# Routing weights broadcast through memory, and the next image's row turns moved in beside the last expert chunks

## The chip, the cores and the metric

The kernel runs on one core of one Trainium2 chip. The metric is the time of one execution in device microseconds (us), as the median of several runs. The profile is of one further execution of the same program and gives its span, from the first instruction to the last. TensorE's granted clock is shown beside it, 1.00 being 2.4 GHz and 0.50 being 1.2 GHz.

## What is computed

Eight images of 56 x 56 tokens with 64 channels pass through two layers. Cut to what matters here:

```python
# layer 0, mixing: y[i] = sum_j relu(xn[i] . xn[j])^2 * t[j], per image
sim = jnp.power(jax.nn.relu(jnp.einsum('bic,bjc->bij', xn, xn)), 2.0)
y = jnp.einsum('bij,bjc->bic', sim, t)
# layer 0, experts: 16 experts of 128, two chosen per token, computed for all tokens
dispatch = jnp.sum(jax.nn.one_hot(top_idx, n_experts) * top_probs[..., None], axis=-2)
hidden = jax.nn.silu(h1) * h2                       # h1, h2: 64 -> 128 for each expert
expert_out = jnp.einsum('bseh,eho->bseo', hidden, w3)
out = jnp.einsum('bseo,bse->bso', expert_out, dispatch)
# layer 1: a deformable 3x3 convolution (nine gathered taps a token, four corners each),
# then a feed-forward layer on the half of the tokens that a router picks, with gelu
```

Each sublayer has a layer norm before it and a skip around it. The routing weights are `dispatch`, one number per token and expert.

## The kernel before, in words

Every engine has an instruction list of its own, written out by hand and run in order. Semaphores tie the lists together (`pe.wait_ge(s["hid_done"], n)` holds the PE list until DVE has made n hidden tiles). The work is in three stages per image `k`:

- **Mixer** (`mixer`, two halves): `sims` makes similarities on PE, `relu_step` on ACT, squares on ACT and DVE, `mix` sums them on PE. It reads the normed rows of image `k` in three channel-major stacks, `xn_hl`, `xn_hh` and `xn_ll` (float16, high and low parts). The geometry of image k-1's convolution (`geo_prepare`), the feed-forward preparation of image k-2 (`ffn_prepare`) and convolution samples are threaded between its steps.
- **Gate**: logits, softmax and the two largest on DVE (`gate`, 26 small steps with drains between), then the feed-forward of image k-2. At its end DVE splits `disp` into a high and a low float16 half (`dsplit`, L891 to L893), PE turns them to channel-major rows (25 transposes in 7 groups) and ACT copies these into `dT` (L1482).
- **Experts** (`experts_chunk`): the 3136 tokens go in 7 chunks `c` (512, 384, 512, 384, 512, 384, 448 tokens), 16 experts `e` in each. Step `e` of the PE list waits for `hid_done` of expert `e`, issues `up(e + 2)` (four matmuls into banks S), a convolution sample's piece of image k-1 at even steps, and at odd steps the down matmuls of an expert pair (L1543 `PS<-work,w3s`), then `spread(p + 1)` (one matmul with `pick` that repeats two experts' routing weights over 64 rows each, into bank Y1) and `collect(p - 1)` (L1747, transposes that accumulate the weighted output into D1). Step `e` of the ACT list does `silu(e)` (L1435), a sample's copy, and at odd steps copies Y1 to `share` (L1441). Step `e` of the DVE list makes `hid(e)` (L908), at odd steps multiplies the pair's output by `share` (`scale_pair`, L904), and weighs gathered corners (`weigh`, L490 to L498). Pieces of the next image's norm (`norm_piece`) fill both lists.

`up(e + 2)` writes the banks that `hid(e)` has read, so PE runs up to two experts ahead of DVE:

```python
for e in range(E):
    pe.wait_ge(s["hid_done"], n0 + e + 1)
    if e + 2 < E:
        up(e + 2, c)
```

After the last chunk, `stacks` turns image k+1's normed rows: 21 groups of 3 or 4 transposes on PE (75 in all) through four banks, and 21 copies on ACT (`evac_tr`, L1281). Beside it DVE runs `geo_start(k)`: row sum, mean, centring, square and row sum over all 25 tiles (L458, L510, L645, L647, L458). The next `mixer` follows. Gathers for the convolution are issued by POOL (L452, nine a tile, two tile buffers `G`). SP issues the other DMAs: the corner table of image k-1, the stored skip of image k-2, the load of image k+1 and the store of `yw`, each behind its own semaphore.

## Time and profile before

| | |
|---|---|
| median of 3 runs | 4166.61 us (4163.04 to 4169.43) |
| profiled execution, span of the core | 4159.1 us |
| profiled execution, time outside the span | not recorded; the median run is 7.5 us above the span |
| mean granted TensorE clock | 0.900 |
| PE, DVE, ACT, POOL busy | 85%, 74%, 58%, 47% of the span |
| experts of image 1 | 663.7 to 880.4 us |
| turning of image 2's rows | 880.4 to 890.1 us |

The middle images repeat with a period of about 461.5 us: the experts of image 1 start at 663.7 and its last collect ends near 880.4, and the same places of image 2 lie near 1125 and 1342. A row's first number is the start, its second the duration; "[0.89 <-DVE work L908]" says that the engine was idle 0.89 us before and that DVE's L908 ended it. A busy PE is a PE with matmuls in flight, and matmuls overlap, so a matmul's slot is the distance to the next start.

### The profile page before, as it was taken

How to read it: one execution, taken by the hardware profiler on the slowest of the kernel's cores; microseconds unless marked ns; L12 is line 12 of the kernel's file. 1: busy time of each engine (PE TensorE's matmuls, PEld its weight loads, DVE VectorE, ACT ScalarE, POOL GpSimd, SP SyncE). 2: the span in 40 equal slices, each digit the busy share in tenths (PEclk: the TensorE clock that was granted, in tenths of full speed). 3: DMA queues.
4: the chain of work that ended last, by engine and by line, in shares of the span. 5: the costliest groups of instructions: out<-in, count | busy, mean ns of one | idle time of the engine just before them, and what ended most of it. 6: DMA issues, size and time to landing. Idle time of an engine off the chain costs nothing.

```text
span 4159.1 us, 58338 instructions
## 1 busy us (share of the span) xinstructions
PE 3515.1 (85%) x21688; PEld 1896.4 (46%) x21688; DVE 3096.5 (74%) x4894; ACT 2399.5 (58%) x4152; POOL 1974.2 (47%) x1805
## 2 busy tenths in 40 slices
PE   5979997999899999999889999999899999946431
PEld 2434444454544445444544455444544455525321
DVE  6466477887788687877788678877688678865775
ACT  5755774577655775577556775577556775522210
POOL 0000074554456364555455463545455464657670
PEclk8989998999899999999899989999899989965555
DMA  4000122232222332231222332232222332234355
GB/s 112 1 8 1 40 82 67 74 99 56 71 83 80 78 89 64 75 98 58 79 77 74 79 96 56 77 92 64 74 79 70 81 86 65 83 103 117 101 123 113
DMA packets 374811, 314.92 MB, mean 76 GB/s; under 512 B 312672, under 2 KB 317024, under 8 KB 374528
## 3 DMA queue, kind: packets, MB, share of 16 engines
q0 software_dynamic: 85248, 231.33, 19.0%
q1 hardware_dynamic: 289280, 79.88, 8.9%
q8 instruction: 171, 2.80, 0.3%
q14 instruction: 112, 0.92, 0.1%
HBM read 279.30 MB, written 57.69 MB: 81 GB/s over the span
## 4 chain that ended last, share of the span: by engine, by line
PE 63%; DVE 16%; ACT 9%; DVEq 5%; issue 3%; DMA 2%; SPq 1%; POOL 1%; ACTq 0%
PE PS L1543 57%; DVE work L908 3%; PE PS L1747 3%; DVEq L492 3%; DVE G L496 2%; PE PS L1579 2%; DVE G L490 2%; DVE small L904 1%; ACT work L1363 1%; ACT work L1435 1%; ACT small L1408 1%; PE PS L1583 1%; ACT xn_hl L1281 1%; POOL G L452 1%; DMA out<-x 1%
## 5 line engine op out<-in xcount | busy, mean ns | idle before, releaser
L452 POOL DMA_INDIRECT G<-corner_table,index x1800 | 1973.6, 1096 | 2049.0 <-DVE values L498 737.5
L1435 ACT ACTIVATE work<-PS,descale 128x512 f32<-128x512 f32 (+2 forms) x896 | 566.7, 633 | 514.9 <-PE PS L1543 503.5
L1363 ACT ACTIVATE work<-PS 128x768 f32<-128x768 f32 (+2 forms) x800 | 651.1, 823 | 273.4 <-PE PS L1543 222.6
L908 DVE SCALAR_TENSOR_TENSOR work<-PS,descale,work 128x512 f32<-128x512 f32 (+2 forms) x896 | 605.7, 680 | 152.3 <-ACT work L1435 138.3
L818 DVE TENSOR_TENSOR work<-work 128x768 f32<-128x768 f32 (+2 forms) x496 | 480.1, 972 | 294.9 <-PE PS L1543 252.4
L1543 PE MATMUL PS<-work,xm 128*64 128x400 f32 (+3 forms) x3200 | 622.3, 502 | 0.0
L490 DVE TENSOR_TENSOR G<-G,corner_w 128x768 f32<-128x768 f32 x600 | 561.4, 951 | 43.5 <-DMA G<-corner_table,index 42.1
L1543 PE MATMUL PS<-xn_hl,xn_hh 128*128 128x384 f16 (+2 forms) x1600 | 539.2, 337 | 51.0 <-ACT work L1363 42.3
L1543 PE MATMUL PS<-xn_hl,xn_ll 128*128 128x384 f16 (+2 forms) x1600 | 534.0, 334 | 0.0
L1543 PE MATMUL PS<-work,w3s 128*64 128x384 f32 (+2 forms) x1792 | 439.8, 569 | 64.5 <-DVE small L904 64.5
L1543 PE MATMUL PS<-xn_hl,w1h 128*128 128x512 f16 (+2 forms) x896 | 319.5, 357 | 64.2 <-DVE work L908 55.6
L1441 ACT ACTIVATE small<-PS 128x512 f32<-128x512 f32 (+2 forms) x448 | 242.9, 542 | 214.4 <-PE PS L1543 211.5
L1543 PEld LDWEIGHTS PS<-xn_hl,xn_hh 128*128 128x128 f16 (+1 forms) x1600 | 158.3, 99 | 379.1 <-ACT work L1363 187.8
L1543 PEld LDWEIGHTS PS<-work,xm 128*64 128x64 f32 (+1 forms) x3200 | 232.1, 136 | 192.8 <-issue 159.0
L1543 PE MATMUL PS<-xn_hl,w2h 128*128 128x512 f16 (+2 forms) x896 | 318.1, 355 | 0.0
L1543 PE MATMUL PS<-xn_hl,w1l 128*128 128x512 f16 (+2 forms) x896 | 318.1, 355 | 0.0
L1543 PE MATMUL PS<-xn_hl,w2l 128*128 128x512 f16 (+2 forms) x896 | 317.8, 355 | 0.0
L904 DVE TENSOR_TENSOR small<-PS,small 128x512 f32<-128x512 f32 (+2 forms) x448 | 275.5, 615 | 31.0 <-PE PS L1543 31.0
L496 DVE TENSOR_TENSOR G<-G 128x1152 f32<-128x1152 f32 x200 | 272.6, 1363 | 18.2 <-issue 0.4
L1287 ACT ACTIVATE val_cm<-PS 128x512 f32<-128x512 f32 x200 | 118.1, 591 | 283.8 <-PE PS L1579 283.8
L1392 ACT ACTIVATE work<-work 128x768 f32<-128x768 f32 (+3 forms) x304 | 259.7, 854 | 2.6 <-PE PS L1543 2.2
L1579 PE MATMUL PS<-ident,values 128*128 128x128 f32 x800 | 139.0, 303 | 142.1 <-DVE xB L503 112.5
(262 smaller groups left out, 4961.2 us busy)
## 6 DMA issues: line engine op xcount, KB each, us to landing
G<-corner_table,index POOLq DMA_INDIRECT x1800
corner_table<-rows_scratch SPq DMA_DIRECT2D x32, 784.0 KB
corner_table<-G SPq DMA_DIRECT2D x8, 841.0 KB, 8.5
xin<-x SPq DMA_DIRECT2D x8, 768.0 KB, 5.7
rows_scratch<-xln SPq DMA_DIRECT2D x8, 768.0 KB
x_scratch<-xB SPq DMA_DIRECT2D x8, 768.0 KB
yw_scratch<-yw SPq DMA_DIRECT2D x7, 784.0 KB, 6.4
x<-x_scratch SPq DMA_DIRECT2D x4, 784.0 KB, 6.0
```

What stands on the lines that cost most here:

```text
L452: GP.indirect_dma_start(G[0:rows, n % 2, tap * 4 * C:(tap + 1) * 4 * C], None, tables[b % 2], bass.IndirectOffsetOnAxis(ap=index[0:rows, c ...
L490: V.tensor_tensor(g, g, bc(w, 2, C), ALU.mult)
L496: V.tensor_tensor(g[:, :, 0:2, :], g[:, :, 0:2, :], g[:, :, 2:4, :], ALU.add)
L818: V.tensor_tensor(sq[0:rows, u % 4, :, 0:n], relu[0:rows, u % 2, :, 0:n], relu[0:rows, u % 2, :, 0:n], ALU.mult).then_inc(s["sq_dve"], 1)
L904: V.tensor_tensor(scaled_y[:, p % 2, 0:w], Y0[:, 0:w], share[:, p % 2, 0:w], ALU.mult).then_inc(s["scaled_done"], 1)
L908: V.scalar_tensor_tensor(hid[:, e % 4, 0:w], S[2 + e % 2][:, 0:w], descale[:, MOE2:MOE2 + 1], silu[:, e % 2, 0:w], ALU.mult, ALU.mult).the ...
L1363: A.activation(relu[0:rows, u % 2, :, 0:n], PS[u % 2][0:rows, :, 0:n], ACT.Relu).then_inc(s["relu_done"], 1)
L1392: A.activation(sq[0:rows, u % 4, :, 0:n], relu[0:rows, u % 2, :, 0:n], ACT.Square).then_inc(s["sq_act"], 1)
L1435: A.activation(silu[:, e % 2, 0:w], S[e % 2][:, 0:w], ACT.Silu, scale=descale[:, MOE1:MOE1 + 1]).then_inc(s["silu_done"], 1)
L1441: A.activation(share[:, e // 2 % 2, 0:w], Y1[:, 0:w], ACT.Copy, scale=1.0 / XS).then_inc(s["share_ready"], 1)
L1543: return P.matmul(o, a, b, start=start, stop=stop, skip_group_check=True)
L1579: ins = P.transpose(D0[:, i * TP:(i + 1) * TP], value[:, i * 128:(i + 1) * 128], ident[0:TP, 0:TP])
```

## The change

Two things are changed.

**Routing weights.** `spread`, `pick`, `dsplit` and the ACT copies of Y1 are gone. PE turns `disp` itself, in float32 (25 `P.transpose`), ACT copies it to `share_cm` (16 rows), SP stores that to DRAM in two pieces (`share_out`) and, for each of the 56 expert pairs of an image, loads two rows back, each broadcast over 64 partitions (`share_back`, two DMAs of up to 128 KB), into four buffers in turn; a buffer is loaded again when `scale_pair` four pairs earlier is done. DVE's `scale_pair` waits for these DMAs. The scale of the up product moves into the routing weight, so `hid` is a two-operand multiply.

**Row turns.** The 21 groups of the next image are no longer behind the last chunk. Group `i` stands at one step (chunk, expert) of `STACK_STEPS`: two in chunk 4, twelve in chunk 5, seven in chunk 6. PE issues it after `up(e + 2)` and the sample's piece, into bank Y1, and ACT copies it at the end of its own step `e`. The token rows have two buffers (`token_cm`), by the image's parity. The first two `sims` of the next image come before the last `collect`. `geo_start` is split: three of four quarters of sum, centring and squares lie in chunks 5 and 6 (the squares on ACT), the last quarter after the last chunk.

```diff
+STACK_STEPS = ((4, 13), (4, 15), *((5, e) for e in (1, 2, 3, 5, 6, 7, 9, 10, 11, 13, 14, 15)), *((6, e) for e in (1, 2, 3, 5, 6, 7, 9)))
@@ SP
+            def share_back(k, p):
+                c, e, n = p // (E // 2), 2 * (p % (E // 2)), k * (NCH * E // 2) + p
...
+                if n >= 4:
+                    sp.wait_ge(s["scaled_done"], n - 3)
+                for b in range(2):
+                    sp.dma_start(share[n % 4][b * C:(b + 1) * C, 0:width(c)],
+                                 share_dram[e + b:e + b + 1, span(c)].to_broadcast([C, width(c)])).then_inc(share_in[n % 4], 16)
@@ SP, image(k)
+                share_out(k)
+                for p in range(NCH * E // 2):
+                    share_back(k, p)
+                    if k >= 2 and p == E // 2 - 1:
+                        store_yw(k - 2)
@@ DVE
+                    if (c, e) == ((5, 2), (5, 6), (5, 8))[q]:
+                        geo_sum(i, quarter(q))
+                    if (c, e) == ((5, 10), (5, 14), (6, 0))[q]:
+                        geo_center(i, q)
+                    if (c, e) == ((6, 6), (6, 8), (6, 10))[q]:
+                        ln_square_sum("g", i, tmp, 0, q)
...
             def geo_start(i):
...
+                geo_sum(i, quarter(3))
+                geo_center(i, 3)
...
-                tt(disp[:, :, :], o1, o2, ALU.add)
-                V.tensor_copy(dsplit[:, :, 0:E], disp[:, :, :])
-                dve.drain()
-                V.tensor_tensor(dsplit[:, :, E:2 * E], disp[:, :, :], dsplit[:, :, 0:E], ALU.subtract).then_inc(s["disp_split"], 1)
+                V.tensor_tensor(disp[:, :, :], o1, o2, ALU.add).then_inc(s["disp_done"], 1)
...
-                    V.scalar_tensor_tensor(hid[:, e % 4, 0:w], S[2 + e % 2][:, 0:w], descale[:, MOE2:MOE2 + 1], silu[:, e % 2, 0:w],
-                                           ALU.mult, ALU.mult).then_inc(s["hid_done"], 1)
+                    V.tensor_tensor(hid[:, e % 4, 0:w], S[2 + e % 2][:, 0:w], silu[:, e % 2, 0:w], ALU.mult).then_inc(s["hid_done"], 1)
@@ ACT, experts_chunk: behind silu(e) and a sample's copy
-                    if e % 2:
-                        act.wait_ge(s["share_done"], p0 + e // 2 + 1)
-                        A.activation(share[:, e // 2 % 2, 0:w], Y1[:, 0:w], ACT.Copy, scale=1.0 / XS).then_inc(s["share_ready"], 1)
...
+                    if k + 1 < B and (c, e) in STACK_STEPS:
+                        i = STACK_STEPS.index((c, e))
...
+                        evac_stack(k + 1, i, Y1)
@@ ACT, image(k), behind the experts
-                if k + 1 < B:
-                    stacks(k + 1, 0, 3 * NCH)
-                ln_std("g", k, 0)
+                square("g", k, tmp, xln, 3)
@@ PE, experts_chunk
+                    if k + 1 < B and (c, e) in STACK_STEPS:
+                        next_stack(k + 1, STACK_STEPS.index((c, e)))
...
-                        pe.wait_ge(s["share_ready"], p0 + p + 1)
-                        if p + 1 < E // 2:
-                            spread(p + 1, c)
...
-                    spread(0, c + 1)
-                    up(0, c + 1)
+                    up(k, 0, c + 1)
+                elif k + 1 < B:
+
+                    pe.wait_ge(s["n_cm"], (k + 2) * 3 * NCH)
+                    sims(k + 1, 0, 0, 0)
+                    sims(k + 1, 0, 0, 1)
@@ PE, gate
-                        ins = mm(S[c % 4][0:2 * E, i * TP:i * TP + rows], dsplit[0:rows, t, :], ident16[0:rows, 0:rows])
+                        ins = P.transpose(S[c % 4][0:E, i * TP:i * TP + rows], disp[0:rows, t, :], ident[0:rows, 0:rows])
```

The PE list of image 1, chunk 5, steps 6 and 7, before (`xn_hl,w1h` begins an up, `work,w3s` is the down, `ident,small` the collect; lines and queues have other numbers in the changed file):

```order
L1543 MATMUL PS0<-xn_hl,w1h 128x384 [waits hid_done]
L1543 MATMUL PS0<-xn_hl,w1l 128x384
L1543 MATMUL PS1<-xn_hl,w2h 128x384
L1543 MATMUL PS1<-xn_hl,w2l 128x384
L1543 MATMUL PS2<-work,w3s 64x384 [waits scaled_done]
L1543 MATMUL PS2<-work,w3s 64x384
L1543 MATMUL PS2<-xn_hh,pick 128x384 [waits share_ready]
L1747 MATMUL PS3<-ident,small 128x128 x3
```

and with the change, both steps (`ident16,split` is a group of row turns):

```order
L1604 MATMUL PS0<-token_cm1,w1h 128x384 [waits hid_done]
L1604 MATMUL PS0<-token_cm1,w1l 128x384
L1604 MATMUL PS1<-token_cm1,w2h 128x384
L1604 MATMUL PS1<-token_cm1,w2l 128x384
L1604 MATMUL PS2<-ident16,split 128x128 [waits n_cm,n_split]
L1604 MATMUL PS2<-ident16,split 128x128 x3
L1604 MATMUL PS0<-token_cm1,w1h 128x384 [waits hid_done]
L1604 MATMUL PS0<-token_cm1,w1l 128x384
L1604 MATMUL PS1<-token_cm1,w2h 128x384
L1604 MATMUL PS1<-token_cm1,w2l 128x384
L1604 MATMUL PS2<-ident16,split 128x128 [waits n_cm,n_split]
L1604 MATMUL PS2<-ident16,split 128x128 x3
```

A group of turns now stands between a step's up and the next step's wait for `hid_done`, and the spread is gone. (The first fence is step 7 alone; step 6 was its first four rows.)

The ACT list at the same place (silus are `work<-PS0,descale`), from the group of step 6 to the silu of step 10, with the change:

```order
L1332 ACTIVATE token_cm0<-PS2 128x512 [waits n_tr]
L1493 ACTIVATE work<-PS0,descale 128x384 [waits up_done]
L1332 ACTIVATE xn_stacks<-PS2 128x512 [waits n_tr]
L1493 ACTIVATE work<-PS0,descale 128x384 [waits up_done] x2
L1332 ACTIVATE xn_stacks<-PS2 128x512 [waits n_tr]
L1493 ACTIVATE work<-PS0,descale 128x384 [waits up_done]
```

Each copy of a group lies between the silu of its own step and the silu of the next.

The PE list at the end of image 1's last chunk, with the change (`zero16` opens the mixer):

```order
L1604 MATMUL PS0<-token_cm0,xn_stacks 128x384 [waits n_cm]
L1604 MATMUL PS0<-token_cm0,xn_stacks 128x384 x3
L1604 MATMUL PS1<-token_cm0,xn_stacks 128x384 x4
L1811 MATMUL PS3<-ident,small 128x128 [waits scaled_done]
L1811 MATMUL PS3<-ident,small 128x128 x2
L1811 MATMUL PS3<-ident,small 64x128
L1604 MATMUL PS2<-zero16 128x384 x2
```

Before, the last collect came first, then the 75 turns, then these similarities.

## Rows read from the trace of the kernel before

**Rows 1.** The page, section 1: busy time, share of the span, instructions.

```profile
PE 3515.1 (85%) x21688; PEld 1896.4 (46%) x21688; DVE 3096.5 (74%) x4894; ACT 2399.5 (58%) x4152; POOL 1974.2 (47%) x1805
```

**Rows 2.** Image 1's experts: busy PE, PEld, DVE, ACT, POOL, PEclk, DMA; waits.

```profile
663.00:880.00 217.00, 201.46 (x1135) 103.61 (x1136) 188.41 (x295) 119.93 (x212) 121.78 (x118) 0.98 0.24 72
...
PE PS L1543 <- DVE small L904: 8.7, 7, 2.6
PE PS L1543 <- DVE work L908: 5.9, 10, 0.9
```

**Rows 3.** Instruction groups, PE: spread, gate's turns (busy us, mean ns, idle before).

```profile
L1543 PE MATMUL PS<-xn_hh,pick 128*128 128x512 f16 (+2 forms) x448 | 163.5, 365 | 0.0
...
L1543 PE MATMUL PS<-ident,dsplit 128*32 128x128 f16 (+1 forms) x200 | 19.9, 261 | 31.9 <-DVE dsplit L893 30.9
```

**Rows 4.** Timeline, PE, image 1, chunk 5, steps 6 to 8.

```profile
835.39 0.33 PE L1543 MATMUL PS<-xn_hl,w1h 128*128 128x384 f16 x1
...
836.04 0.33 PE L1543 MATMUL PS<-xn_hl,w1h 128*128 128x384 f16 x1
...
837.58 0.34 PE L1543 MATMUL PS<-xn_hh,pick 128*128 128x384 f16 x1
837.76 0.49 PE L1747 MATMUL PS<-ident,small 128*128 128x128 f32 x3
838.09 0.33 PE L1543 MATMUL PS<-xn_hl,w1h 128*128 128x384 f16 x1
```

**Rows 5.** Timeline, same chunk, ACT and DVE: a silu, its hid, a scale_pair.

```profile
841.17 0.55 DVE L904 TENSOR_TENSOR small<-PS,small 128x384 f32<-128x384 f32 x1
...
842.06 0.58 ACT L1435 ACTIVATE work<-PS,descale 128x384 f32<-128x384 f32 x1 [0.49 <-PE PS L1543]
...
842.68 0.62 DVE L908 SCALAR_TENSOR_TENSOR work<-PS,descale,work 128x384 f32<-128x384 f32 x1
```

**Rows 6.** Timelines of PE, ACT and DVE, from image 1's experts to image 2's mixer.

```profile
880.39 8.58 PE L1543 MATMUL PS<-ident,split 128*128 128x128 f16 x75
890.14 0.34 PE L1543 MATMUL PS<-xn_hl,xn_hh 128*128 128x384 f16 x1 [1.17 <-ACT xn_ll L1281]
...
880.81 0.60 ACT L1281 ACTIVATE xn_hl<-PS 128x512 f16<-128x512 f32 x1 [1.58 <-PE PS L1543]
881.31 0.59 ACT L1281 ACTIVATE xn_hh<-PS 128x512 f16<-128x512 f32 x1
...
882.26 0.51 ACT L1281 ACTIVATE xn_hl<-PS 128x384 f16<-128x384 f32 x1
882.63 0.53 ACT L1281 ACTIVATE xn_hh<-PS 128x384 f16<-128x384 f32 x1
...
891.00 1.51 ACT L1363 ACTIVATE work<-PS 128x768 f32<-128x768 f32 x2 [0.81 <-PE PS L1543]
...
881.60 1.82 DVE L458 TENSOR_REDUCE st<-xB 128x25 f32<-128x1600 f32 x1
```

**Rows 7.** Timelines at image 1's gate: PE, DVE.

```profile
659.95 2.90 PE L1543 MATMUL PS<-ident,dsplit 128*32 128x128 f16 x25 [15.44 <-DVE dsplit L893]
663.74 0.61 PE L1543 MATMUL PS<-xn_hl,w1h 128*128 128x512 f16 x1 [0.89 <-ACT xn_hh L1482]
...
658.68 0.57 DVE L891 CAST dsplit<-small 128x400 f16<-128x400 f32 x1
```

**Rows 8.** Busy by stretch around a lull of PE inside image 1's mixer.

```profile
499.90:503.30 3.40, 1.12 (x8) 0.31 (x4) 0.50 (x2) 3.33 (x13) 0.00 (x0) 1.00 0.00 0
503.30:506.70 3.40, 3.32 (x22) 1.18 (x22) 2.09 (x5) 2.38 (x4) 0.00 (x0) 0.50 0.00 0
```

**Rows 9.** A 128 KB load; POOL's waits in 663 to 880; DVE in the tail.

```profile
work<-pick_in SPq DMA_DIRECT2D x1, 128.0 KB, 2.4
...
POOL G L452 <- DVE values L498: 72.5, 14, 27.1
...
3684.97 2.70 DVE L490 TENSOR_TENSOR G<-G,corner_w 128x768 f32<-128x768 f32 x3 [9.18 <-DMA G<-corner_table,index]
```

More of the change, by code:

```diff
@@ L636, in nothing, with geo_sum, geo_center, geo_early @@
             def nothing(): pass
-            def geo_start(i):
-                x2 = xB[i % 2]
-                dve.drain()
-                ln_sum(x2[:, :, :], 0)
-                ln_mean(0)
-                if i > 0:
-                    dve.wait_ge(s["rows_written"], i * 32)
-                V.tensor_tensor(xln[:, :, :], x2[:, :, :], bc(st[:, 0, 1, :], 2, C), ALU.subtract)
-                dve.drain()
-                V.tensor_tensor(tmp[:, :, :], xln[:, :, :], xln[:, :, :], ALU.mult)
-                dve.drain()
-                red(st[:, 0, 2, :], tmp[:, :, :])
-                ln_var("g", 0, LNC_EPS)
+            def geo_sum(i, r):
+                dve.drain()
+                red(st[:, 0, 0, r], xB[i % 2][:, r, :])
+            def geo_center(i, q):
+                r = quarter(q)
+                if q in (0, 3):
+                    all_in = slice(0, quarter(2).stop) if q == 0 else r
+                    dve.drain()
+                    V.tensor_scalar(st[:, 0, 1, all_in], st[:, 0, 0, all_in], 1.0 / C, None, ALU.mult)
+                    dve.drain()
+                if q == 0 and i > 0:
+                    dve.wait_ge(s["rows_written"], i * 32)
+                ln_center("g", xln, xB[i % 2], 0, q)
+            def geo_early(i, c, e):
+                for q in range(3):
+                    if (c, e) == ((5, 2), (5, 6), (5, 8))[q]:
[4 more added lines that the diff above has]
+                        ln_square_sum("g", i, tmp, 0, q)
+            def geo_start(i):
+                geo_sum(i, quarter(3))
+                geo_center(i, 3)
             def ffn_sum(f):
@@ L1329, in offsets_tm, with geo_early @@
                 taken(slice(18, 27), ACT.Sigmoid).then_inc(s["om_taken"], 1)
+            def geo_early(i, c, e):
+                for q in range(3):
+                    if (c, e) == ((5, 15), (6, 1), (6, 3))[q]:
+                        square("g", i, tmp, xln, q)
             def geo_prepare(i, j, u):
+                if (j, u) == (0, 0):
+                    ln_std("g", i, 0)
                 for q in range(4):
-                    if (j, u) == ((0, 1), (0, 2), (0, 4), (0, 7))[q]:
+                    if (j, u) == ((0, 2), (0, 4), (0, 5), (0, 7))[q]:
                         cast_h("g", i, 0, q)
@@ L1450, in gelu_chunk, with evac_stack @@
                                  bias=fb1c[:, m:m + 1], scale=descale[:, FFN1:FFN1 + 1]).then_inc(s["gelu_done"], 1)
-            def stacks(k, i0, i1):
-                for i in range(i0, i1):
-                    c = i // 3
-                    evac_tr("n", k * 3 * NCH, i, (xn_hl, xn_hh, xn_ll)[i % 3][:, span(c)], S[i % 4][:, 0:width(c)])
+            def evac_stack(k, i, bank):
+                c = i // 3
+                evac_tr("n", k * 3 * NCH, i, (normed(k), xn_hh, xn_ll)[i % 3][:, span(c)], bank[:, 0:width(c)])
             def image(k):
@@ L1481, in image @@
                     act.wait_ge(s["disp_tr"], k * NCH + c + 1)
-                    A.activation(dT[0:2 * E, span(c)], S[c % 4][0:2 * E, 0:width(c)], ACT.Copy).then_inc(s["disp_cm"], 1)
+                    A.activation(share_cm[:, span(c)], S[c % 4][0:E, 0:width(c)], ACT.Copy).then_inc(s["disp_cm"], 1)
                 for c in range(NCH):
@@ L1556, in transpose_map, with first_stacks, next_stack @@
                 ins.then_inc(s["g_tr"], 1)
-            def stacks(k, i0, i1):
-                if i0 == 0:
-                    pe.wait_ge(s["n_split"], 4 * k + 4)
-                for i in range(i0, i1):
+            def first_stacks():
+                pe.wait_ge(s["n_split"], 4)
+                for i in range(3 * NCH):
                     if i >= 4:
-                        pe.wait_ge(s["n_cm"], k * 3 * NCH + i - 3)
+                        pe.wait_ge(s["n_cm"], i - 3)
                     transpose_chunk("n", S[i % 4], i // 3, (C, 0, 2 * C)[i % 3])
-                if i1 == 3 * NCH:
-                    pe.wait_ge(s["n_cm"], (k + 1) * 3 * NCH)
+                pe.wait_ge(s["n_cm"], 3 * NCH)
+            def next_stack(k, i):
+                if i == 0 and k >= 3:
+                    pe.wait_ge(s["fout_read"], k - 2)
+                pe.wait_ge(s["n_split"], 4 * k + quarters_of(i // 3))
+                if i:
+                    pe.wait_ge(s["n_cm"], k * 3 * NCH + i)
+                transpose_chunk("n", Y1, i // 3, (C, 0, 2 * C)[i % 3])
             def sample(b, t, stage):
@@ L1653, in ffn_prepare, with sims @@
                         ffn_transpose(f, c)
-            def sims(half, j, u):
+            def sims(k, half, j, u):
                 rows, n = tile_rows(j), IWS[half]
```

121 lines of the change are left out of this document (67 added, 54 removed).

## The prediction, made before the change was run

> **What bounds the kernel now.** I read the page first [rows 1]: PE is busy 85% of the span, DVE 74%, ACT 58%, POOL 47%. PE leads, but a share over the whole span does not say what an edit of one stage is worth, so I went to the stage that is changed. In the experts of image 1 [rows 2] PE is busy 201 of 217 us at a clock of 0.98, DVE 188, ACT 120. PE's waits there are 8.7 + 5.9 us, so the stage lasts as long as PE's instruction slots. DVE is close behind. The timeline of two steps shows the same [rows 4]: step 6 takes 836.04 - 835.39 = 0.65 us, which is its four up matmuls back to back; step 7 takes 838.09 - 836.04 = 2.05 us and holds up, down, spread and collect without a pause that another engine ends. PE can run so because the ups are two experts ahead: silu and hid of the next expert are made while PE does this one. Between the experts and the next mixer, PE, ACT and DVE all change work [rows 6]: the turns start at 880.39, the first similarities at 890.14, the first relu at 891.00.
>
> **The change, part by part.** An execution of 4159.1 us is the base; the median of the runs shown is 7.5 us above it.
>
> *Spread.* 448 matmuls go [rows 3]. One slot at 384 columns is 837.76 - 837.58 = 0.18 us [rows 4], by columns 0.22 at 512, on average 0.20. Fourteen of an image's 56 lie in steps that also get a group of turns and are priced there; the 42 others give 8.2 us in each of images 0 to 6 and the last image gives 10.9: 68 us. PE is the bound but DVE's 188 of 217 us is near [rows 2], so I count 85% of it, **-58 us**. The ACT copies of Y1 lie beside PE work, and go at no gain. Hid loses an operand and goes from 0.62 to about the 0.55 of a two-operand multiply of that size [rows 5]; DVE is not the bound, so that is worth nothing where PE leads.
>
> *Turns inside the steps.* Here I expect the loss. The group of step e is issued after up(e + 2). ACT copies it at the end of its own step e, so ahead of silu(e + 1); hid(e + 1) waits for silu(e + 1); and PE's step e + 1 begins with a wait for hid(e + 1). The two-expert lead is gone in such a step, and the engines take turns. The length of one such round, for 384 tokens: up 0.65 [rows 4]; from the group's first transpose to the start of its copy 880.81 - 880.39 = 0.42 [rows 6]; from that copy to the next ACT instruction 0.50 at 512 columns and 0.37 at 384 [rows 6]; silu 0.58, then 842.68 - 842.64 = 0.04 to hid, hid 0.55, and 0.04 again to PE [rows 5]. That is 2.78 us, or 2.60 with a group of three tiles (0.37 + 0.37 in place of 0.42 + 0.50), half of each in chunk 5: 2.69. It is 2.04 more than an even step and 0.64 more than an odd one, spread included. Chunk 5 has groups at even steps 2, 6, 10, 14 and odd steps 1, 3, 5, 7, 9, 11, 13 that pay (15 hides in the wait at the chunk's end): 8.2 + 4.5 = 12.7 us. Chunk 6 has two even and five odd: 4.1 + 3.2 = 7.3. In chunk 4 only step 13 pays, about 0.4. That is 20.3 us an image and, for the seven images that have a next one, **+142 us**. Sample pieces lengthen a step on both sides alike. The step after such a row (4, 8, 12) has lost its lead as well: DVE must weigh (0.90 each, 2.70 for three [rows 9]) and make hid, some 1.5 us, where PE needs 0.8; about 1.5 us an image, **+9 us**.
>
> *Boundary.* The 9.75 us between 880.39 and 890.14 go. What is late next is the geometry's last quarter: after the last collect DVE adds the output twice (it takes until 881.60, when the row sum starts [rows 6]), then a quarter of sum and centring, about 0.6 each by a quarter of 1.82 plus the start, and a small step; ACT squares, 0.6, and only then takes the first relu. So relu starts near 883.7. The eight similarities now ahead of the last collect push it by 0.9. The relu comes 891.0 - 884.6 = 6.4 us earlier, seven times, **-45 us**. But PE then has nothing for some 3 us. In the mixer of image 1 a stretch of 3.4 us with 1.1 us of PE work was followed by 3.4 us at clock 0.50 [rows 8], and 3.4 us at half clock is at most 1.7 us of lost work: **+12 us** for seven. After image 7 the shorter geo_start (it now makes a quarter of it in place of all: four passes of 1.82 [rows 6], 7.3 us, become about 2.5) lies on the path to the tail: **-5 us**.
>
> *Gate.* In float32 a turn has a slot of (838.09 - 837.76) / 3 = 0.11 us at full clock [rows 4], twice that at half: 2.75 or 5.5 us for 25, against 2.90 before [rows 7] and some 3.1 for ACT's copies beside them. The two DVE steps for dsplit (658.68 to 659.95, 1.27 us) go, but PE waited for them 30.9 us in all [rows 3], 15.4 of it in image 1, so in images 0 and 1 alone. I take +0.9 for each of these two and +0.3 for the six others: **+4 us**.
>
> *Broadcasts.* 56 pairs an image, two loads of up to 128 KB each. One load of 128 KB took 2.4 us [rows 9]. A pair is wanted every 2.7 to 3.9 us and four buffers lie ahead, so a pair has over 10 us: nothing on the path. SP has little else to issue meanwhile. The bounds are from nothing to 2.4 us more on each of 56 pairs, far off. What could be hit is the gathers: POOL waited 72.5 us of 217 for DVE [rows 9], so that much slack covers them; I take 0. The Trainium skill ("DMA: Bandwidth & Descriptors", section "Issuing engines are not separate DMA queues") says that DMAs of all issuers share the same 16 engines and interleave. By that rule the broadcasts slow the gathers; the trace agrees in the tail, where the table's write held DVE for 9.18 us on a gather [rows 9]. It is a rival below.
>
> *Clock in the rounds.* PE is at work in about half of a round, less in even steps. If the clock stays at 1.00 this costs nothing; if it is at 0.50 all through, each of 21 rounds has up and turns twice as long, +0.85 us, 125 us for seven images. The stretch in [rows 8] was emptier (a third) than a round, so I stay near the lower end: **+12 us**.
>
> Sum: -58 + 142 + 9 - 45 + 12 - 5 + 4 + 12 = **+71 us**, 4230 for the profiled execution's span and 4238 against the median.
>
> **The rivals.**
> 1. *The rounds don't form* (faster). PE would need a copy that finds ACT idle and a silu that does not wait, so that a group costs only its own slots, at most 0.42 us by 21 groups, under 9 us an image. Then: spread -87 (all of it), turns at most +55, boundary and clock -33, tail and gate -1: 66 less, 4100. For it speaks that ACT is busy only 120 of 217 us; against it the two lists, in which the copy stands ahead of silu(e + 1). It decides when a round costs less than half of my 0.97 us mean excess: 147 rounds by 0.48 are 71 us. That half-way case is no change.
> 2. *Gathers are late.* The experts move 72 GB/s at a DMA share of 0.24 [rows 2]; the broadcasts add some 12.8 MB in 217 us, 59 GB/s. In the tail at a high share a gather came 9 us late [rows 9]. If one of two tiles an image-chunk comes 2 us late beyond POOL's slack, 14 tiles an image by 2 us by 3 to 7 images: 60 to 100 more, about 4320.
> 3. *Half clock in the rounds*, as worked out: 4238 + 113 = about 4350.
> 4. *The first pair of an image is late*, by at most two DMAs of 2.4 us each way: under 5 us by 8. It only widens the range.
>
> **How the numbers follow.** My forecast has 0.68, rival 1 0.13 (with 0.06 more for the half-way case), rival 2 0.06, rival 3 0.07. What a measurement here can tell from no change is 0.2%, 8 us. Slower: 0.68 + 0.06 + 0.07 = 0.81; same 0.05; faster 0.14, part of the half-way case being on either side. The forecast's own range is 4205 to 4280 (85 to 100% of the spread, rounds between 2.5 and 2.9 us, clock between 0 and 40 us). To hold 8 in 10 the range goes down to 4160, the half-way case, and up to 4305; it leaves out rival 1 and the upper part of 2 and 3.
>
> **What would show it.** In the changed profile: PE steps of chunk 5 that carry a group near 2.7 us, with PE idle before each up and DVE's hid named as what ended it, and chunk 5 some 13 us longer than before; chunks 0 to 3 shorter by 1 to 1.7 us each; first relu about 4 us behind the last collect, PEclk at 0.50 just after; no DVE wait for share DMAs. I am wrong if chunk 5 keeps its length (rival 1), if weigh waits for gathers in the experts (rival 2), or if PEclk in chunks 5 and 6 is far below 1 (rival 3).

## The result, and the profile after

The changed kernel takes 4253.3 us (median of 4 runs, 4248.7 to 4261.5) against 4168.0 us (4 runs, 4163.0 to 4170.9): ratio 1.0205, 95% interval 1.019 to 1.0221, so 79 to 92 us slower. Forecast were 4238 us and 71 us slower, in a range of 4160 to 4305.

Section 1 of the changed kernel's page answers to [rows 1]; under it the rows on clock and DMA (tenths, 40 slices) and on the hardware queue's share:

```profile
PE 3497.6 (82%) x21240; PEld 1876.7 (44%) x21240; DVE 3021.2 (71%) x4948; ACT 2174.2 (51%) x3736; POOL 1971.7 (46%) x1805
...
PEclk8989998999899999999899998999899999965555
DMA  4021124432353333432353333432353333443445
...
q1 hardware_dynamic: 361424, 184.17, 17.3%
```

Every engine has less to do than before, PE too, and the span is 90.7 us longer (4249.9 against 4159.1). So the loss is waiting, not work. The waits of the whole run name it, of PE before:

```profile
PE PS L1543 <- DVE small L904: 64.5, 56, 3.0
PE PS L1543 <- DVE work L908: 55.6, 89, 1.2
```

and after (L961 is the line that makes `hid`, L908 before):

```profile
PE PS L1604 <- DVE work L961: 177.2, 203, 2.0
...
PE PS L1604 <- ACT work L1422: 62.9, 59, 3.7
PE PS L1604 <- DVE small L957: 58.5, 55, 2.6
```

(A row of waits gives the total in us, the number of waits and the longest.) PE waits for `hid` 203 times in place of 89, and 177.2 us in place of 55.6. To see where, I cut both spans at the starts of PE's `w1h` matmuls, of which there is one for each image, chunk and expert. The forecast's terms are put beside the stages they belong to (the gate's term lies between the images); differences are of unrounded times:

| stage, us | before | after | difference | forecast |
|---|---|---|---|---|
| chunks 0 to 4, eight images | 1249.0 | 1206.4 | -42.6 | -49 |
| chunk 5, eight images | 213.6 | 323.1 | +109.4 | |
| chunk 6 to its last up, eight images | 197.4 | 269.3 | +71.9 | 5 and 6: +154 |
| from there to the next image's first up, seven | 1741.2 | 1697.0 | -44.2 | -29 |
| head and tail | 758.0 | 754.1 | -3.8 | -5 |

The round itself. Timelines of PE, ACT and DVE of the changed kernel, image 1, chunk 5, from up(8) to up(9), an even step with a group:

```profile
845.81 0.34 PE L1604 MATMUL PS<-token_cm,w1h 128*128 128x384 f16 x1 [0.37 <-DVE work L961]
...
846.47 0.39 PE L1604 MATMUL PS<-ident,split 128*128 128x128 f16 x4
848.61 0.34 PE L1604 MATMUL PS<-token_cm,w1h 128*128 128x384 f16 x1 [1.75 <-DVE work L961]
...
846.90 0.60 ACT L1332 ACTIVATE token_cm<-PS 128x512 f16<-128x512 f32 x1 [1.73 <-PE PS L1604]
847.39 0.57 ACT L1493 ACTIVATE work<-PS,descale 128x384 f32<-128x384 f32 x1
...
848.00 0.56 DVE L961 TENSOR_TENSOR work<-PS,work 128x384 f32<-128x384 f32 x1 [1.60 <-ACT work L1493]
```

Up from 845.81, turns from 846.47, copy at 846.90, silu at 847.39, hid at 848.00, PE again at 848.61: 2.80 us, where the same step took 0.65 before [rows 4]. PE waits for DVE, DVE for ACT and ACT for PE, so the five pieces of this chain follow one another and none lies beside another. The forecast had 2.78 for this round and 2.60 with three tiles; the latter measures 2.64 (median of images 1 to 6; 843.18 to 845.81 in this one).

The boundary, which answers to [rows 6]: PE, ACT and DVE after the last chunk of image 1.

```profile
911.33 0.60 PE L1811 MATMUL PS<-ident,small 128*128 128x128 f32 x4
911.77 0.49 PE L1604 MATMUL PS<-zero 128*128 128x384 f16 x2
915.91 1.36 PE L1604 MATMUL PS<-token_cm,xn_stacks 128*128 128x384 f16 x7 [3.65 <-ACT work L1422]
...
914.58 0.58 ACT L1323 ACTIVATE tmp<-xln 128x448 f32<-128x448 f32 x1 [6.09 <-DVE xln L550]
915.06 1.49 ACT L1422 ACTIVATE work<-PS 128x768 f32<-128x768 f32 x2
...
912.97 0.62 DVE L493 TENSOR_REDUCE st<-xB 128x7 f32<-128x448 f32 x1
913.67 0.17 DVE L684 TENSOR_SCALAR st<-st 128x7 f32<-128x7 f32 x1
913.92 0.63 DVE L550 TENSOR_TENSOR xln<-xB,st 128x448 f32<-128x448 f32 x1
```

The first relu (915.06) is 3.13 us behind the end of the last collect (911.33 + 0.60). Before, the last collect of image 1 was

```profile
879.89 0.66 PE L1747 MATMUL PS<-ident,small 128*128 128x128 f32 x4 [0.20 <-DVE small L904]
```

and the relu at 891.00 [rows 6] was 10.45 behind its end. The chain between is the one forecast: two additions, the quarter's sum, its mean, its centring, ACT's square, relu.

### The profile page after: what moved, and what is told of

The parts are those of the page before. It is cut to its first block, busy times and chain, and to the rows that moved or that the text cites. A ratio compares the mean times of both kernels' runs of the same rounds, so it can differ in the third digit from the quotient of the medians.

```text
span 4249.9 us, 58165 instructions
## 1 busy us (share of the span) xinstructions
PE 3497.6 (82%) x21240; PEld 1876.7 (44%) x21240; DVE 3021.2 (71%) x4948; ACT 2174.2 (51%) x3736; POOL 1971.7 (46%) x1805
## 4 chain that ended last, share of the span: by engine, by line
PE 58%; DVE 18%; ACT 10%; DVEq 5%; issue 4%; DMA 2%; POOL 1%; SPq 1%; ACTq 0%
PE PS L1604 52%; DVE work L961 5%; PE PS L1811 3%; DVEq L527 3%; ACT work L1493 2%; DVE G L525 2%; DVE G L531 2%; PE PS L1647 2%; DVE small L957 1%; POOL G L487 1%; ACT token_cm L1332 1%; ACT work L1422 1%; ACT xn_stacks L1332 1%; DVE st L493 1%; ACT small L1467 1%
## 5 line engine op out<-in xcount | busy, mean ns | idle before, releaser
L961 DVE TENSOR_TENSOR work<-PS,work 128x512 f32<-128x512 f32 (+2 forms) x896 | 551.7, 619 | 299.0 <-ACT work L1493 294.6
L1604 PE MATMUL PS<-token_cm,xn_stacks 128*128 128x400 f16 (+3 forms) x3200 | 628.6, 338 | 63.6 <-ACT work L1422 62.9
L1604 PEld LDWEIGHTS PS<-token_cm,xn_stacks 128*128 128x128 f16 (+1 forms) x3200 | 286.2, 100 | 478.4 <-ACT work L1422 208.1
L1604 PE MATMUL PS<-token_cm,w1h 128*128 128x512 f16 (+2 forms) x896 | 325.7, 363 | 155.4 <-DVE work L961 148.4
L1604 PE MATMUL PS<-token_cm,w1l 128*128 128x512 f16 (+2 forms) x896 | 323.0, 361 | 0.0
L1604 PE MATMUL PS<-token_cm,w2h 128*128 128x512 f16 (+2 forms) x896 | 321.9, 359 | 0.0
L1604 PE MATMUL PS<-token_cm,w2l 128*128 128x512 f16 (+2 forms) x896 | 320.8, 358 | 0.0
L1811 PEld LDWEIGHTS PS<-ident,small 128*128 128x128 f32 x1600 | 178.5, 145 | 304.7 <-issue 297.2
L1811 PE MATMUL PS<-ident,small 128*128 128x128 f32 x1600 | 282.8, 297 | 0.2 <-DVE small L957 0.2
L1604 PE MATMUL PS<-ident,split 128*128 128x128 f16 (+1 forms) x1224 | 143.0, 241 | 116.4 <-DVE split L1223 48.4
```

What stands on the lines that cost most here:

```text
L961: V.tensor_tensor(hid[:, e % 4, 0:w], S[2 + e % 2][:, 0:w], silu[:, e % 2, 0:w], ALU.mult).then_inc(s["hid_done"], 1)
L1604: return P.matmul(o, a, b, start=start, stop=stop, skip_group_check=True)
L1811: ins = P.matmul(D1[0:rows, n * 128:(n + 1) * 128], scaled_y[:, p % 2, n * TP:n * TP + rows], ident[:, :], start=p == 0 and n == 0, stop=p ...
```

## The experiments

Eleven kernels, each timed beside the kernel before on the same chip; the ratios are against that timing (medians of 4165.2 to 4170.5 us). The stages are those of the table above (head and tail, 750 to 761 us, left out). They are of the one profiled execution, which is not always the median one: with the copy one step later it took 4079.2 us, the shortest of four, with copy later and geometry at the end 4117.9, the longest.

| run | median, us | ratio to before | chunks 0 to 4 | chunk 5 | chunk 6 | between |
|---|---|---|---|---|---|---|
| before | 4168.0 | | 1249.0 | 213.6 | 197.4 | 1741.2 |
| changed kernel | 4253.3 | 1.019 to 1.0221 | 1206.4 | 323.1 | 269.3 | 1697.0 |
| copy one step later | 4088.9 | 0.9794 to 0.9827 | 1188.1 | 233.2 | 206.3 | 1700.1 |
| turns at the end | 4117.2 | 0.9857 to 0.989 | 1189.8 | 221.0 | 197.1 | 1754.5 |
| routing weights alone | 4098.9 | 0.9795 to 0.9853 | 1185.9 | 204.7 | 189.4 | 1758.2 |
| geometry at the end | 4274.6 | 1.0238 to 1.0272 | 1204.8 | 321.9 | 264.6 | 1727.4 |
| no broadcasts | 4262.8 | 1.0191 to 1.0242 | 1203.8 | 320.9 | 275.1 | 1710.3 |
| odd steps | 4218.3 | 1.0096 to 1.0138 | 1216.8 | 278.5 | 253.0 | 1713.4 |
| odd steps, copy later | 4087.4 | 0.9789 to 0.9824 | 1193.5 | 226.4 | 202.4 | 1705.4 |
| turns ahead of up | 4148.0 | 0.9944 to 0.9976 | 1194.8 | 260.2 | 224.8 | 1703.6 |
| copy later, geometry at the end | 4114.7 | 0.9858 to 0.9899 | 1188.3 | 230.8 | 202.4 | 1733.5 |
| geometry moved, first | 4096.9 | 0.9802 to 0.9841 | 1189.3 | 242.7 | 203.1 | 1708.4 |
| geometry moved, second | 4092.1 | 0.9806 to 0.9848 | 1187.9 | 232.3 | 205.7 | 1707.1 |

**The copy one step later.** ACT's copy of step e's group moves behind silu(e + 1); PE and DVE are as in the changed kernel.

```diff
-                    if k + 1 < B and (c, e) in STACK_STEPS:
-                        i = STACK_STEPS.index((c, e))
+                    if k + 1 < B and (c - (e == 0), (e - 1) % E) in STACK_STEPS:
+                        i = STACK_STEPS.index((c - (e == 0), (e - 1) % E))
```

> The changed kernel, but ACT copies the group of step e one step later, behind silu(e + 1) in place of ahead of it. Theory of the rounds (copy ahead of silu(e + 1) takes PE's lead away): chunks 5 and 6 of images 0 to 6, 181 us longer than before in the changed kernel, keep only the groups' own slots and the geometry's passes, some 40 to 60 us; steps with a group fall from 2.6 to 2.8 us to about 1.1 (even) and 2.3 (odd); in all 4253 - 130 = about 4125 us. Rival (a group costs its price wherever the copy stands: PE slots, a lower clock, DVE): within 30 us of 4253.

Measured 4088.9 us: 164 us less than the changed kernel and 79 us less than before. I had expected 128 less: chunks 5 and 6 keep 28.5 us over before, not 40 to 60, and chunks 0 to 4 give another 18 back, 16 of them in chunk 4. Of the 164 us an estimated 19 to 34 are the clock, which no longer falls in chunks 5 and 6 (worked out below). The same step in its trace, from up(8) to up(9), and a step on:

```profile
812.94 0.34 PE L1604 MATMUL PS<-token_cm,w1h 128*128 128x384 f16 x1
...
813.60 0.39 PE L1604 MATMUL PS<-ident,split 128*128 128x128 f16 x4
814.05 0.34 PE L1604 MATMUL PS<-token_cm,w1h 128*128 128x384 f16 x1
...
816.26 0.33 PE L1604 MATMUL PS<-token_cm,w1h 128*128 128x384 f16 x1
...
814.03 0.60 ACT L1332 ACTIVATE token_cm<-PS 128x512 f16<-128x512 f32 x1 [1.48 <-PE PS L1604]
...
813.45 0.55 DVE L961 TENSOR_TENSOR work<-PS,work 128x384 f32<-128x384 f32 x1
```

The hid that PE needs for its next step starts at 813.45, while PE is still in this one, and up(9) follows the turns with no wait: 1.11 us in place of 2.80. The odd step takes 2.21 (814.05 to 816.26), and 1.92 is an odd step's length with neither spread nor group (same chunk, routing weights alone). So a group costs 0.46 and 0.29 us here, about its slots, and no round forms. PE's waits for hid over the run fall back to what they were before:

```profile
PE PS L1604 <- DVE work L961: 57.5, 92, 1.2
```

One position in ACT's list is thus the whole loss, and more: the other parts of the change are a gain.

**Turns at the end; routing weights alone.** The first takes `next_stack` and `evac_stack` out of the steps and puts them behind the last chunk, through four banks (PE's part is shown; ACT's copies move likewise):

```diff
                 for c in range(NCH):
                     experts_chunk(k, c)
+                if k + 1 < B:
+                    pe.wait_ge(s["n_split"], 4 * k + 8)
+                    for i in range(3 * NCH):
+                        if i >= 4:
+                            pe.wait_ge(s["n_cm"], (k + 1) * 3 * NCH + i - 3)
+                        transpose_chunk("n", S[i % 4], i // 3, (C, 0, 2 * C)[i % 3])
+                    pe.wait_ge(s["n_cm"], (k + 2) * 3 * NCH)
+                    sims(k + 1, 0, 0, 0)
+                    sims(k + 1, 0, 0, 1)
```

> The changed kernel with all 21 groups of row turns back behind the last chunk, through four banks; the geometry's passes stay in the steps, the weights still go through memory. Rounds theory: chunks 5 and 6 lose their 181 us and gain the spread's slots (20 us) less the geometry's passes on DVE (about 16 us); the boundary takes back some 7 us seven times, 50 us: 4253 - 181 - 4 + 50 = about 4115 us. If the weights' way through memory cost something (gathers late, waits for the loads) this would stay above 4150.

The second does so as well and has the geometry at the end too:

```diff
             def geo_start(i):
-                geo_sum(i, quarter(3))
-                geo_center(i, 3)
+                for q in range(4):
+                    geo_sum(i, quarter(q))
+                for q in range(4):
+                    geo_center(i, q)
...
-                square("g", k, tmp, xln, 3)
+                for q in range(4):
+                    square("g", k, tmp, xln, q)
```

> As the run before, and the geometry's four sums, centrings and squares also back behind the last chunk: what is left of the change is the weights' way through memory. By my terms (spread -58, gate measured at -4) about 4168 - 62 = 4106 us, so a little below the run before (its geometry passes cost 2.3 us in chunk 5 of the last image, where there are no turns; times eight is 18, less 3 in the tail). If geometry passes are free in the steps, this run is no faster than the one before or slower.

Measured 4117.2 and 4098.9 us, expected 4115 and 4106. With the routing part alone, chunks 0 to 6 are 80.0 us shorter than before: 0.179 us for each of the 448 spreads, 90% of the slot of 0.20. What lies between the images is 17 us longer there, and why is not shown. Half of it stands in the gate, where in both kernels the clock is low for some 27 us an image; over all that lies between the images, the clock rows hold 290 us at half clock against 254 before, which may be a part of it. The two runs also bring out a cost that the forecast did not have: with the geometry's passes in the steps, chunks 5 and 6 are 24.0 us longer (221.0 + 197.1 against 204.7 + 189.4). In the first of the two, images 1 to 6 also have 3.4 us each at half clock in these chunks, the second has none, so some us of the 24 are the clock's.

From here the row turns' account can be made without the rest. Against the kernel with the turns at the end, the changed one has +191 us in the steps (+16.6, +102.1, +72.2) and -57.5 between the images: +133. With the later copy it is +20 in the steps and -54 between: -35 (-28 by the medians).

**Geometry at the end**, the turns left in the steps (the diff is the second one above, on the changed kernel):

> The changed kernel with the geometry's sums, centrings and squares all behind the last chunk; the turns stay in the steps. First relu later: three more quarters of sum and centring on DVE, 3.6 us, and ACT's squares, so the boundary is about 3.5 us longer, seven times, and the tail 5 us: +30. Against it, chunk 5 loses the passes: -16 if they are on the path beside the rounds, 0 if the rounds hide them. So 4267 (on the path) or 4283 us (hidden).

Measured 4274.6 us, 21 more, half-way between the two expected. The first relu is 3.7 us later, seven times, 26.2 us; chunks 5 and 6 together are 5.9 us shorter. So the rounds hide most of the passes, and these make up some 6 us of the loss at most.

**No broadcasts** from image 1 on:

```diff
-                    share_back(k, p)
+                    if k == 0:
+                        share_back(k, p)
...
-                    dve.wait_ge(share_in[n % 4], 32 * (n // 4 + 1))
+                    if k == 0:
+                        dve.wait_ge(share_in[n % 4], 32 * (n // 4 + 1))
```

> The changed kernel with the broadcasts and DVE's waits for them left out from image 1 on (the weights of images 1 to 7 are then stale values of the four buffers, so the routing weights are wrong in them). If the 12.8 MB an image hide beside the rest, as forecast: within 8 us of 4253. If they hold up the gathers (rival 2): faster by 20 us or more, and POOL's gathers and DVE's wait for them shorter.

Measured 4262.8 us (4250.7 to 4267.3): not faster, with 90 MB less to move. (The two intervals overlap; its profiled execution has 21 us more at half clock in chunks 5 and 6, and 31 more between the images.) Its page and a row of POOL's waits in the experts of image 1 (676 to 911), then the same wait of the changed kernel there:

```profile
q1 hardware_dynamic: 298704, 94.20, 10.0%
...
POOL G L488 <- DVE values L534: 85.6, 12, 26.6
```

```profile
POOL G L487 <- DVE values L533: 90.8, 13, 26.4
```

POOL waits for DVE about as long with the broadcasts as without, so it has slack in both. The gathers do land a little later: from the issue of a tile's last gather to the last landing the median of 200 tiles is 3.18 us in the changed kernel, 2.84 without broadcasts and 2.93 before. POOL's slack covers these 0.3 us. The offsets that steer the gathers are worked out from wrong values in this run, so its gathers may read other addresses; the kernel before, with the right ones, gives nearly the same figure. A broadcast of 128 KB took 3.2 us from issue to landing, the four buffers give it over 10, and DVE never waits for one in the changed kernel's trace.

**Odd steps.** The order on ACT is that of the changed kernel, but 19 of the 21 groups stand in odd steps in place of 15:

```diff
-STACK_STEPS = ((4, 13), (4, 15), *((5, e) for e in (1, 2, 3, 5, 6, 7, 9, 10, 11, 13, 14, 15)), *((6, e) for e in (1, 2, 3, 5, 6, 7, 9)))
+STACK_STEPS = (*((4, e) for e in (9, 11, 13, 15)), *((5, e) for e in (1, 3, 5, 7, 8, 9, 11, 13, 15)), *((6, e) for e in (1, 3, 5, 7, 8, 9, 11, 13)))
```

> The changed kernel, ACT's copy still ahead of the next silu, but 19 of the 21 groups at odd steps (from step 9 of chunk 4 on) in place of 15. Rounds theory: a round is 2.6 to 2.8 (3.05 in chunk 6) whatever the step, so four fewer even steps (0.65 to 2.8) and four more odd ones (2.05 to 2.8) are worth 4 x 1.4 x 7 = 39 us: about 4215 us. A fixed price of a group: no change, within 10 us of 4253.

Measured 4218.3 us, for 4215 by the theory of the rounds. The steps bear it out: in chunk 5 an odd step with a group now takes 2.63 to 2.80 us (medians of images 1 to 6) and the one even step (step 8) went from 1.10 to 3.24. A round is as long wherever it forms, and in an odd step more of it was there already. That the total fits so well is luck in part: the steps lost 50 us and the stretches between the images gained 16, and chunks 5 and 6 have 10 us at half clock in place of 86, which the theory had left out. A fixed price for a group, with the clock's gain added, would give nearly the same total; the lengths of the steps and the next run speak against it.

**Odd steps and the later copy** together:

> The odd steps of the run above and the later copy together. In the later-copy kernel an even step with a group is 0.46 us longer than one without, an odd one 0.3 to 0.46; so where a group stands should matter no more once no round forms: within 12 us of the later-copy kernel's 4089. Rival (even steps are dearer for another reason, such as DVE's work in them): 20 us or more below it.

Measured 4087.4 against 4088.9 us, no difference. Once no round forms, the place of a group does not matter.

**Turns ahead of up.** ACT as in the changed kernel; on PE the group goes ahead of the step's up:

```diff
                     pe.wait_ge(s["hid_done"], n0 + e + 1)
+                    if k + 1 < B and (c, e) in STACK_STEPS:
+                        next_stack(k + 1, STACK_STEPS.index((c, e)))
                     if e + 2 < E:
                         up(k, e + 2, c)
...
-                    if k + 1 < B and (c, e) in STACK_STEPS:
-                        next_stack(k + 1, STACK_STEPS.index((c, e)))
```

> The changed kernel, ACT's copy still ahead of silu(e + 1), but PE issues the group of a step ahead of up(e + 2) in place of behind it. Rounds theory: the up (0.65) then runs beside the copy, and the round from hid to hid is turns 0.42 + copy 0.50 + silu 0.58 + 0.04 + hid 0.55 + 0.04 = 2.13 us. An even step with a group goes from 2.8 to about 2.15, an odd one is again bound by PE's own slots, about 2.35: six even groups by 0.65 and fourteen odd ones by 0.35 are 8.8 us an image, 62 us: about 4190. If what holds the next step were not this chain but, say, the group's wait for its bank, the order of the two would not matter: within 10 us of 4253.

Measured 4148.0 us: 105 less than the changed kernel, where I expected 62. Timelines of PE, ACT and DVE of the same even step:

```profile
825.43 0.40 PE L1604 MATMUL PS<-ident,split 128*128 128x128 f16 x4
825.66 0.33 PE L1604 MATMUL PS<-token_cm,w1h 128*128 128x384 f16 x1
...
827.58 0.40 PE L1604 MATMUL PS<-ident,split 128*128 128x128 f16 x4 [1.10 <-DVE work L961]
827.81 0.33 PE L1604 MATMUL PS<-token_cm,w1h 128*128 128x384 f16 x1
...
829.74 0.33 PE L1604 MATMUL PS<-token_cm,w1h 128*128 128x384 f16 x1
...
825.86 0.60 ACT L1332 ACTIVATE token_cm<-PS 128x512 f16<-128x512 f32 x1 [1.48 <-PE PS L1604]
826.36 0.57 ACT L1493 ACTIVATE work<-PS,descale 128x384 f32<-128x384 f32 x1
...
826.96 0.56 DVE L961 TENSOR_TENSOR work<-PS,work 128x384 f32<-128x384 f32 x1 [0.95 <-ACT work L1493]
```

The round is turns, copy, silu, hid, 825.43 to 827.58: 2.15 us, forecast 2.13, with the up now beside the copy. The odd step behind it takes 2.16, from its own group at 827.58 to the next step's up at 829.74, where I had 2.35. Fourteen such steps by 0.19 are an estimated 19 us over seven images; that, and the clock (below, an estimated 15 to 30 us), is why it gained more.

**Geometry at the end with the later copy:**

> The later-copy kernel with the geometry's sums, centrings and squares all behind the last chunk. Its two prices are known from runs: in the steps they cost 24 us where no rounds hide them, behind the last chunk they hold the first relu up by 3.7 us seven times, 26 us. So no difference from the later-copy kernel, within 10 us of 4089; chunks 5 and 6 shorter by about 3 us an image, the relu later by 3.7.

Measured 4114.7 us, 26 more: a miss. The 24 us that the passes cost with the turns at the end are 6 here (chunk 5 2.4, chunk 6 3.9), and there is no half clock in these chunks in either run. Between the images 33 us come in the two profiled executions, 26 of them the later relu. A price found beside one neighbour did not hold beside another. Why is not shown; that PE's slots for the turns cover DVE's passes would fit.

**The geometry's passes moved** to where DVE was seen idle, on the later-copy kernel, twice. The first move (the second is ((5, 3), (5, 6), (5, 11)), ((6, 0), (6, 2), (6, 3)), and ((6, 1), (6, 4), (6, 5)) on ACT):

```diff
-                    if (c, e) == ((5, 2), (5, 6), (5, 8))[q]:
+                    if (c, e) == ((5, 3), (5, 4), (5, 11))[q]:
...
-                    if (c, e) == ((5, 10), (5, 14), (6, 0))[q]:
+                    if (c, e) == ((5, 12), (6, 2), (6, 3))[q]:
...
-                    if (c, e) == ((6, 6), (6, 8), (6, 10))[q]:
+                    if (c, e) == ((6, 10), (6, 11), (6, 12))[q]:
...
-                    if (c, e) == ((5, 15), (6, 1), (6, 3))[q]:
+                    if (c, e) == ((5, 15), (6, 4), (6, 5))[q]:
```

> The later-copy kernel with the geometry's nine DVE passes moved to steps 3, 4, 11 and 12 of chunk 5 and 2, 3, 10, 11 and 12 of chunk 6, ahead of which or behind which its trace shows DVE idle. If these passes are on the path because DVE is busy in the steps they stand in (24 us by the two runs with the turns at the end): 10 to 20 us below 4089. If DVE is the bound of the whole stretch, so that it does not matter where they stand: within 8 us.

> The later-copy kernel with the geometry's DVE passes moved a second time: sums behind steps 3, 6 and 11 of chunk 5, centrings behind 0, 2 and 3 and sums of squares behind 10, 11 and 12 of chunk 6. The first move took 0.4 us off chunk 6 of each image and put 0.7 and 0.9 us on the two steps that follow steps 4 and 12 of chunk 5; without those: chunk 5 shorter by 1 to 2 us an image, chunk 6 by 0.4, so 10 to 15 us below 4089. If any place on DVE costs the same: 4089.

Measured 4096.9 and 4092.1 us, no gain either time; their intervals overlap that of the later-copy kernel. So the first expectation, 10 to 20 us less, and that of the second move, 10 to 15 less, both missed. The first move put 0.68 and 0.89 us (mean of images 1 to 6) on the intervals after up(6) and up(14) of chunk 5, where it had placed a pass ahead of hid 5 and hid 13, and made chunk 5 9.5 us longer in all. The second came out level in both chunks (232.3 for 233.2, 205.7 for 206.3), since the passes cost only some 6 us there in all, as the run before this one shows. There was little left to win.

## Why the prediction was right

*What bounds the kernel, and the round.* Right, and shown: 2.80 us for 2.78, 2.64 for 2.60. Moving the copy behind the silu takes 164 us away, and moving the up beside the copy shortens the round to 2.15 for 2.13. Four groups moved from even to odd steps are worth 35 us where 1.4 us each gave 39, though part of that agreement is luck, as said there. The excess of an even step, 2.15 us (0.65 to 2.80) for 2.04, was right as well.

*Where the term was too small.* Chunks 5 and 6 cost +181 us for +154, chunk 4 some +2.4 us an image for +0.4. Three causes are visible, and the geometry's passes, which the forecast had at nothing in the steps, are some 6 us more by the run with the geometry at the end.

First, the clock. Windows of the changed kernel: chunk 5 and chunk 6 of image 1, chunk 5 of image 2 (columns as in [rows 2], PEclk third from the end).

```profile
828.48:870.13 41.65, 30.26 (x194) 16.95 (x193) 26.47 (x45) 15.99 (x33) 16.39 (x18) 0.95 0.32 92
870.13:905.38 35.25, 29.10 (x163) 15.59 (x162) 21.56 (x36) 13.71 (x27) 16.22 (x18) 0.91 0.33 99
1305.76:1349.55 43.79, 32.83 (x194) 17.89 (x193) 26.71 (x45) 15.99 (x33) 18.02 (x18) 0.89 0.31 91
```

The same chunks of the later-copy kernel have:

```profile
799.66:829.49 29.83, 27.68 (x195) 16.24 (x193) 26.05 (x46) 16.10 (x33) 19.45 (x19) 1.00 0.49 134
829.49:855.83 26.34, 25.52 (x164) 14.38 (x162) 21.77 (x37) 14.38 (x28) 16.77 (x17) 1.00 0.45 130
```

The granted clock is either 1.00 or 0.50, so 0.95 over 41.65 us is 4.2 us at half and 0.89 over 43.79 is 9.6. The two chunks do the same, and the one with 5.4 us more of half clock is 2.1 us longer: 0.4 us for each. In chunks 5 and 6 of images 0 to 6 the clock rows hold 86 us of half clock (none before, none with the later copy, 10 us with the turns ahead of up), 49 of them in chunk 5. By the price above that makes an estimated 19 us in chunk 5 and at most 15 in chunk 6, where images 1 to 6 show no such price (4.9 us at half go with 35.49 us, 6.4 with 35.25). So it is 19 to 34 us where my term for the clock in the rounds was 12: right in kind, too near its lower end. PE is busy 73% of those 41.65 us, and rival 3 (half clock all through) did not come.

Second, chunk 4. "In chunk 4 only step 13 pays, about 0.4" was wrong. The end of chunk 4 in the changed kernel, PE and DVE:

```profile
821.01 0.39 PE L1604 MATMUL PS<-ident,split 128*128 128x128 f16 x4
...
824.98 0.38 PE L1604 MATMUL PS<-ident,split 128*128 128x128 f16 x4 [1.99 <-DVE work L961]
825.66 1.98 PE L1604 MATMUL PS<-work,w3s 128*64 128x512 f32 x4 [0.30 <-DVE small L957]
...
822.72 0.69 DVE L961 TENSOR_TENSOR work<-PS,work 128x512 f32<-128x512 f32 x1 [1.54 <-ACT work L1493]
823.33 0.95 DVE L643 TENSOR_TENSOR split<-tmp,split 128x768 f16<-128x768 f32 x1
824.19 0.68 DVE L961 TENSOR_TENSOR work<-PS,work 128x512 f32<-128x512 f32 x1
```

At step 13 the last up is out, so nothing lies between the late hid 14 and step 15, and DVE has a split of the next image's rows (0.95) in that chain. PE idles 1.99 us; the stretch from up(15) to the next chunk takes 7.98 us in the mean of images 1 to 6, against 5.55 with the later copy. Seven times 2.4 are 17 us.

Third, smaller sizes: I priced the odd steps from 2.05, but step 1, which has no collect, took 1.73 before and 2.80 after in chunk 5, +1.07 in place of +0.64, and 1.96 and 3.43 in chunk 6, where with the geometry at the end it took 3.02. And in chunk 6, of 448 columns, a round is 3.05, not 2.69; an even step there was 0.76, so +2.29 for +2.04.

*Spread.* Forecast -58 at 85% of a slot; the routing part alone shows 90%, -80 us over the 448. Chunks 0 to 4 alone are 63 us shorter there; the changed kernel keeps 43 of them, 16.6 us being lost in chunk 4, and chunks 0 to 3 have 21 us at half clock for 10. ACT's copies and DVE's shorter multiply were costed at nothing, and nothing in the runs contradicts that; no run takes the spread's 80 us apart from them.

*Boundary.* Exact: the relu came 10.45 - 3.13 = 7.32 us closer to the last collect, and the similarities ahead of that collect took 1.0 back (last up to end of collect 5.53 before, 6.55 after): 6.3 for 6.4. Most of the clock's +12 did not come. Busy by stretch over the lull of image 1, for [rows 8]:

```profile
911.70:916.00 4.30, 0.65 (x6) 0.25 (x4) 3.00 (x7) 1.42 (x3) 3.08 (x5) 1.00 0.31 96
916.00:926.00 10.00, 9.32 (x61) 4.83 (x60) 9.23 (x15) 8.99 (x17) 4.76 (x4) 1.00 0.23 67
```

Here the clock stayed at 1.00, behind a lull emptier than that of [rows 8]; in each of the six other images a low stretch of 3.4 us or two follow the last collect, 24 us in all. The mixer from the first relu to the last `w_mix` grew by 3.6 us over seven images, with 23 us more at half clock in it (87 for 65), so +12 was an upper bound.

*Gate.* Forecast +4, measured -3.5 from the last `w_mix` to the first up, seven images. In image 1 the 25 turns did take 5.28 us for 2.90, at half clock, as the upper of the two prices had it, and yet three other images came out 2.7 shorter. What lies in the gate shifts by some 3 us with where the clock rises, so the term's sign stays open.

*Broadcasts.* 0 forecast, 0 found, for the two reasons given: four buffers lie ahead, POOL has slack. The reading of the tail was wrong, though. DVE's wait of 9.18 us [rows 9] (9.0 in the changed kernel) is for a tile of nine gathers, whose issues by POOL alone take 11.85 us from the first to the last there; the last then landed in 4.1 us, against a median of 2.93 over the run. So the table's write, and whatever else moved then, explains about 1.2 us of the wait and not 9, and later in the tail DVE waits 4.1 to 6.7 us for gathers that land in 2.7 to 2.8 us. Rival 2's price of 2 us a tile beyond POOL's slack was therefore set from a row that does not show it. The Trainium skill's rule that DMAs of all issuers share the same engines and interleave ("DMA: Bandwidth & Descriptors", "Issuing engines are not separate DMA queues") fits what the trace has, gathers 0.3 us later beside the broadcasts and 1.2 and 2.1 us later in two tiles near the table's write, but it did not decide here: ahead of the tail gathers held DVE for more than 0.3 us four times, 4.0 us in all (once before the change), and taking the broadcasts out made nothing faster.

*Rivals.* "The rounds don't form" is what the kernel becomes with the copy one step later. I had it at 4100, and it takes 4089. In the kernel as changed, the order of ACT's list decided, as I said.

*Slips in the working.* By the forecast's own lists 13 groups (1, 7 and 5) stand in odd steps that pay, not 14; that is 1.4 us of spread. Rival 1's turns, at most 9 us in seven images, are 62 and not 55. Rival 3's 0.85 us a round has no working; twice the up's 0.65 and the group's 0.42 would be up to 1.07 more.

*Luck.* The total came out close, 79 to 92 us for 71, partly because errors offset each other: +27 in chunks 5 and 6 and +6 in chunks 0 to 4 against -15 between the images, where most of the clock's +12 and the gate's +4 did not show.

## What to carry to other kernels

Where work runs two stages ahead, ask of an added piece not whether each engine has room for it, but where in each list it stands against the instruction that keeps the lead. Here ACT was busy 55% of the experts before the change [rows 2] and the copy took 0.5 us; one place too early, ahead of the silu and waiting for PE's newest work, it serialised three engines, 2.8 us a step. With a step of delay for this consumer of fresh work, it cost about its slots here. And price a chain by adding starts to starts from the trace: the round of 384 tokens came out within 0.04 us of what was worked out from rows of the kernel before.

## What had not been expected of the hardware

The clock: with PE busy 73% of chunk 5, in a round some 1.1 us on and 1.7 off, single stretches of 3.4 us at half clock appear, 7 to 15 us of them in chunks 5 and 6 of an image, and where they fall differs from image to image (PEclk 0.95 in one, 0.89 in the next, with the same instructions), so that chunks with equal work differ by 2.1 us. And a lull of 3.65 us between images (0.65 us of PE in 4.30) was followed by full clock in one image and by a low stretch in the six others, with the same instructions in all seven.

The gathers: 90 MB of broadcasts beside them made them land 0.3 us later (3.18 us for 2.84 without), and with POOL's slack of 91 us in the experts of image 1 this cost no time that the runs can tell.
